# A decoder layer on one core: skip term written into PSUM by ScalarE, four slot products added by GpSimd

## What is computed

```python
xi, z = jnp.split(jnp.einsum('bld,ed->ble', xn, in_proj_w), 2, axis=-1)   # 1024 channels each
xc = silu(conv4(xi) + conv_b)
dt, Bm, Cm = jnp.split(jnp.einsum('bld,ed->ble', xc, x_proj_w), ...)
delta = softplus(dt @ dt_proj_w.T + dt_proj_b)
h[t] = exp(delta[t] * A) * h[t-1] + delta[t] * Bm[t] * xc[t]              # 16 states per channel
y = (h * Cm).sum(states) + xc * Dp                                        # xc * Dp is the skip term
y = y * silu(z);  out = y @ out_proj_w.T
```

## Time and profile before

| | |
|---|---|
| time, median of 3 runs | 2715.13 us (2707.16 to 2716.41) |
| the profiled execution: time, span | 2712.88 us, 2711.1 us |
| start, to the first u of step 0 | 79.6 us |
| 16 steps | 79.6 to about 1957 us |
| steps 4 to 13, each | 118.5 us |
| experts | 2030 to 2711 us |
| busy share of the span: PE, DVE, ACT, POOL | 93%, 78%, 63%, 61% |

### The profile page before, as it was taken

The page is one execution under the profiler, slowest core; times in us unless marked ns, Lnnn a source line. Parts: engine busy times, 40 slices in busy tenths (PEclk is TensorE's granted clock), DMA queues, the critical chain, the costliest instruction groups (busy, mean ns, idle before and its releaser), DMA issues.

```text
span 2711.1 us, 37373 instructions
## 1 busy us (share of the span) xinstructions
PE 2533.4 (93%) x11936; PEld 2179.8 (80%) x11936; DVE 2122.4 (78%) x2360; ACT 1714.0 (63%) x3891; POOL 1661.0 (61%) x980
## 2 busy tenths in 40 slices
PE   5689999999999999999999999998869999999997
PEld 5688888878888787888888788876649999999996
DVE  6899999989999998999899999998933454445442
ACT  4667787877777786877778777786643333333331
POOL 0878888878887988888788888888710100001100
PEclk9899999999999999999999999998879999999999
DMA  7123202122020212202020220202052332433320
GB/s 223 61 77 122 76 22 82 42 63 82 22 76 22 82 39 59 85 26 76 22 82 28 76 82 22 69 22 75 14 181 86 136 121 95 150 119 118 130 93 17
DMA packets 90907, 208.41 MB, mean 77 GB/s; under 512 B 7742, under 2 KB 16574, under 8 KB 90498
## 3 DMA queue, kind: packets, MB, share of 16 engines
q1 hardware_dynamic: 81506, 184.61, 21.6%
q0 software_dynamic: 5120, 14.21, 1.6%
q10 hardware_dynamic: 4096, 7.34, 0.9%
HBM read 176.69 MB, written 29.98 MB: 76 GB/s over the span
## 4 chain that ended last, share of the span: by engine, by line
PE 59%; DVE 13%; issue 9%; POOL 7%; ACT 7%; DMA 3%; SPq 1%; DVEq 0%; POOLq 0%; ACTq 0%
PE y L1511 14%; PE work L1525 12%; PE ring L1525 11%; PE work L1337 11%; DVE ring L1204 6%; POOL arena L929 3%; PE work L1358 3%; DVE arena L1213 3%; PE work L1374 2%; ACT ring L782 2%; DMA arena<-bc_rows 2%; DVE arena L1204 2%; PE work L1348 1%; POOL arena L934 1%; PE y L1508 1%
## 5 line engine op out<-in xcount | busy, mean ns | idle before, releaser
L929 POOL TENSOR_TENSOR arena<-arena 128x896 f32<-128x896 f32 x512 | 1058.5, 2090 | 221.8 <-PE y L1511 186.4
L782 ACT ACTIVATE ring<-arena,small 128x224 f32<-128x224 f32 x2048 | 795.7, 436 | 269.7 <-DVE arena L1213 229.6
L1511 PE MATMUL y<-arena,cst_sb 128*128 128x224 f32 x4096 | 857.5, 360 | 46.0 <-POOL arena L934 25.9
L1204 DVE TENSOR_TENSOR_SCAN ring<-ring,arena 128x896 f32<-128x896 f32 x400 | 809.2, 2023 | 93.1 <-ACT ring L782 51.4
L1511 PEld LDWEIGHTS y<-arena,cst_sb 128*128 128x128 f32 x4096 | 784.5, 194 | 104.0 <-issue 36.9
L947 POOL DMA_INDIRECT out<-res,ids x32 | 48.9, 1528 | 636.4 <-DVE mst L1261 554.1
L1213 DVE TENSOR_TENSOR arena<-ring,arena 128x896 f32<-128x896 f32 x400 | 433.2, 1083 | 5.4
L1337 PE MATMUL work<-arena 128*128 128x224 f32 x1984 | 406.5, 364 | 14.9 <-DVE slot_i L1109 8.9
L1337 PEld LDWEIGHTS work<-arena 128*128 128x128 f32 x1984 | 386.7, 197 | 23.3 <-DVE slot_i L1109 13.6
L1276 DVE SCALAR_TENSOR_TENSOR hidden_lo<-work,hidden_hi 128x448 fp32r<-128x448 f32 x128 | 80.0, 625 | 345.0 <-ACT hidden_hi L832 345.0
L832 ACT ACTIVATE hidden_hi<-work 128x448 fp32r<-128x448 f32 x128 | 69.8, 545 | 369.2 <-PE work L1525 369.2
(11 more groups left out here) (195 smaller groups left out, 3279.8 us busy)
## 6 DMA issues: line engine op xcount, KB each, us to landing
weights<-in_w SPq DMA_DIRECT2D x64, 1024.0 KB, 7.1
arena<-bc_rows SPq DMA_DIRECT2D x128, 448.0 KB, 4.5
arena<-in_ctx SPq DMA_DIRECT2D x16, 896.0 KB, 8.9
expert_rows<-x2e SPq DMA_DIRECT2D x1, 7224.0 KB, 29.8
xrow<-expert_rows SPq DMA_DIRECT2D x8, 903.0 KB, 11.7
arena<-in_xT SPq DMA_DIRECT2D x16, 448.0 KB, 9.5
arena<-in_x SPq DMA_DIRECT2D x16, 448.0 KB, 3.7
out<-arena ACTq DMA_DIRECT2D x32, 224.0 KB, 2.3
```

The source lines that it names most:

```text
L782: last = nc.scalar.activation(decays[s % 2][:, i * L:(i + 1) * L], delta[:, k, :], ACT.Exp, scale=a_neg[:, n:n + 1])
L929: nc.gpsimd.tensor_tensor(u[:, s % 4], dx[:, k:k + 1, :].to_broadcast([P, QN, L]), bc[:, 0, q * QN:(q + 1) * QN, :], ALU.mult).then_inc(u_ ...
L1204: nc.vector.tensor_tensor_scan(states, h, u_flat[:, s % 4, :], 0.0, ALU.mult, ALU.add).then_inc(scan_done, 1)
L1511: last = nc.tensor.matmul(o, ident, u[:, s % 4, i, :], start=False, stop=(q == Q - 1 and i == QN - 1))
```

## The change

1. **Skip term.** The matmuls of L1508, the tile `diag` and the 8 activations that built it in the start go. ACT writes `xc * D` straight into the PSUM bank of a channel pair (`skip_columns`, 2 activations of 128 x 224 for each of 4 pairs: jobs skip0 to skip3), after the gate has read the bank's last contents. PE waits for it (`skip_ready`) before the first sum of the pair, and all its sums accumulate onto it.
2. **Added products.** For slots 5, 9, 13 and 17 (`ADDED`) POOL, after its multiply, adds the product of the slot in front, in place. PE leaves out slots 4, 8, 12 and 16 and raises `sum_done` by two after the slot behind.
3. **A fifth u buffer**: buffer `s % 5` up to slot 19, `s % 4` from slot 20.
4. **Places.** All four tables, some banks and the orders of step -1 are new. In the start DVE's masks0 stands in the middle of the convolution, and ACT's silu stands ahead of the z copies.
5. w_x and w_dt get a semaphore of their own; PE's first xp waits for these two loads only, and others wait for the remaining six.

```diff
+    u_of = [s % 5 if s < 20 else s % 4 for s in range(SLOTS)]
...
+        ADDED = (5, 9, 13, 17)
...
+            def skip_columns(step, par, j):
+                if isinstance(step, int) and step == 0 and j < 2:
+                    act.wait_ge(w_free[2 + j], len(jobs_of[-1][2 + j]))
+                need(act, y_done, step * PAIRS + (j - 1))
+                if j == 0:
+                    act.wait_ge(xc_ready, step + 1)
+                for i in range(2):
+                    k = 2 * j + i
+                    last = nc.scalar.activation(yb[j % 2][:, i * L:(i + 1) * L], xc[:, par, k, :], ACT.Copy, scale=d_skip[:, k:k + 1])
+                last.then_inc(skip_ready, 1)
...
-                    for k in range(KB):
-                        nc.scalar.activation(diag[:, k, :], ident, ACT.Copy, scale=d_skip[:, k:k + 1]).then_inc(s_diag, 1)
...
-                    need(pool, sum_done, b * SLOTS + (s - 3))
+                    last = max((p for p in range(s) if u_of[p] == u_of[s]), default=max(p for p in range(SLOTS) if u_of[p] == u_of[s]) - SLOTS)
+                    need(pool, sum_done, b * SLOTS + (last + 1))
...
+                    if s - 2 in ADDED:
+                        pool.wait_ge(multiplied, b * len(ADDED) + (ADDED.index(s - 2) + 1))
+                        apart(pool)
+                        product_made(pool, b, s - 3)
+                        nc.gpsimd.tensor_tensor(u[:, u_of[s - 2]], u[:, u_of[s - 2]], u[:, u_of[s - 3]], ALU.add
                                                 ).then_inc(pooled_ready, 1)
...
                         if k % 2 == 0:
-                            need(pe, y_done, b * PAIRS + (k // 2 - 1))
-                        nc.tensor.matmul(o, diag[:, k, :], xc[:, par, k, :], start=True, stop=False)
+                            pe.wait_ge(skip_ready, b * PAIRS + (k // 2 + 1))
+                            apart(pe)
+                    if s + 1 in ADDED:
+                        return
                     product_made(pe, b, s)
                     for i in range(QN):
-                        last = nc.tensor.matmul(o, ident, u[:, s % 4, i, :], start=False, stop=(q == Q - 1 and i == QN - 1))
-                    last.then_inc(sum_done, 1)
+                        last = nc.tensor.matmul(o, ident, u[:, u_of[s], i, :], start=False, stop=(q == Q - 1 and i == QN - 1),
+                                                skip_group_check=True)
+                    last.then_inc(sum_done, 2 if s in ADDED else 1)
```

The places that matter below, before and after (the number is the slot):

```diff
-PE_AT   xi0-xi1: 0       xi2: 2         tx, rt, xi3: 3   out0.1-0.3: 7     out1.0: 8      out1.1-1.3: 10   z0, z1, plug: 16   z2, z3: 20
+PE_AT   xi0.0-xi1.0: 0   xi1.1, xi2: 1   tx, rt, xi3: 4   out0.1-out1.1: 7  out1.2-1.3: 9  z0.0-z1.0: 15    plug: 17   z1.1, z2, t1: 20   z3: 23
-POOL_AT delta1, delta2: 4   delta3: 11   scatter: 19   ctx: 20   delta0: 31   xn: 32
+POOL_AT delta1, delta2: 4   delta3: 12   scatter: 24   ctx: 30   delta0: 32   xn: 32.01
+ACT_AT  skip1: 9.01   skip2: 15   skip3: 26   skip0 (of the next step): 31
-DVE_FIRST ... conv2.1 conv2.2 conv2.3 conv3.1 conv3.2 conv3.3 masks0 masks1 ... masks7 corr0 ...
+DVE_FIRST ... conv2.1 masks0 conv2.2 conv2.3 conv3.1 conv3.2 conv3.3 masks1 ... masks7 corr0 ...
```

More of the change, by code:

```diff
@@ L45, in build_decoder @@
     SUB = QN * L
+    UB = 5
+    u_of = [s % 5 if s < 20 else s % 4 for s in range(SLOTS)]
     BIG_STEP = 1e28
@@ L73, in build_decoder @@
         for name, n in (
-            ("bc", 2 * NS * L), ("u", 4 * SUB), ("delta", KB * L), ("dx", KB * L), ("xc", 2 * KB * L),
+            ("bc", 2 * NS * L), ("u", UB * SUB), ("delta", KB * L), ("dx", KB * L), ("xc", 2 * KB * L),
             ("xT", DC * L), ("xn", DC * L), ("w1p", KB * L), ("sp3", 4 * L), ("w_in", DC * 2 * DI), ("gate", 2 * KB * L),
-            ("w_out", KB * D), ("w_x", KB * 3 * R), ("w_xa", DC * D), ("diag", KB * P),
+            ("w_out", KB * D), ("w_x", KB * 3 * R), ("w_xa", DC * D),
             ("x_res", 2 * D), ("r", 2 * D), ("hx", 2 * D), ("hT", 2 * DC * H), ("ctx", 2 * DCTX),
@@ L252, in apart @@
             eng.sem_inc(wait_kept, 1)
[L255 to L258, removed]
[5 rows of a table removed]
-        ACT_AT = {"norm2.0": 0, "tap0": 3, "tap1": 3.01, "norm2.1": 4, "tap2": 4.01, "tx0": 5, "tx1": 5.01, "tap3": 8,
[3 rows of a table removed]
-        DVE_AT = {"norm21.0": 1, "norm21.1": 2, "norm21.2": 3, "conv0.1": 3.01, "conv0.2": 3.02, "conv0.3": 3.03,
[6 rows of a table removed]
+        JOB_BANK = {"xi0": 0, "xi1": 1, "xi2": 0, "xi3": 1, "tx0": 1, "tx1": 0, "rt": 0, "rank": 1, "xp": 0, "out0": 0,
+                    "out1": 1, "dt0": 0, "dt1": 0, "dt2": 1, "dt3": 0, "z0": 1, "z1": 0, "z2": 1, "z3": 0, "t0": 1, "t1": 0,
+                    "plug": 1, "ssq": 1, "xatt0": 0, "xatt1": 1}
+        PE_AT = {"xi0.0": 0, "xi0.1": 0.01, "xi1.0": 0.02, "xi1.1": 1, "xi2.0": 1.01, "xi2.1": 1.02, "tx0": 4, "tx1": 4.01,
[5 rows of a table added]
+        ACT_AT = {"norm2.0": 1, "tap0": 3, "drop0": 3.01, "norm2.1": 4, "tap1": 4.01, "tap2": 4.02, "tx0": 5, "tx1": 5.01,
[3 rows of a table added]
+        DVE_AT = {"mask": 0, "norm21.0": 1, "norm21.1": 1.01, "norm21.2": 2, "conv0.1": 3, "conv0.2": 3.01, "conv0.3": 3.02,
[6 rows of a table added]
                   "norm20.2": 30.02}
-        POOL_AT = {"delta1": 4, "delta2": 4.01, "delta3": 11, "scatter": 19, "ctx": 20, "delta0": 31, "xn": 32}
+        POOL_AT = {"delta1": 4, "delta2": 4.01, "delta3": 12, "scatter": 24, "ctx": 30, "delta0": 32, "xn": 32.01}
         in_order = lambda names: {name: k for k, name in enumerate(names.split())}
@@ L279, in build_decoder @@
                                dt2 dt3 ssq""")
-        ACT_FIRST = in_order("""w_z skip tap0 tap1 tap2 tap3 z0 z1 z2 silu xp square z3 sp0 sp1 sp2 sp3 logs""")
-        DVE_FIRST = in_order("""conv0.1 conv0.2 conv0.3 conv1.1 conv1.2 conv1.3 conv2.1 conv2.2 conv2.3 conv3.1 conv3.2 conv3.3
-                                masks0 masks1 masks2 masks3 masks4 masks5 masks6 masks7 corr0 corr1 corr2 corr3""")
+        ACT_FIRST = in_order("""w_z tap0 tap1 tap2 tap3 silu z0 z1 z2 xp z3 sp0 sp1 sp2 sp3 square logs skip0""")
+        DVE_FIRST = in_order("""conv0.1 conv0.2 conv0.3 conv1.1 conv1.2 conv1.3 conv2.1 masks0 conv2.2 conv2.3 conv3.1 conv3.2
+                                conv3.3 masks1 masks2 masks3 masks4 masks5 masks6 masks7 corr0 corr1 corr2 corr3""")
         PE_DRAIN = in_order("""out0.0 out0.1 tx0 plug out0.2 out0.3 out1.0 out1.1 out1.2 out1.3 tx1 rt t0 rank t1 xatt0.0 xatt0.1
@@ L630, in last_tap @@
                 if j == 0 and (not isinstance(b, int) or b >= 1):
+                    act.wait_ge(skip_ready, b * PAIRS)
+                    apart(act)
                     act.wait_ge(sum_done, b * SLOTS - Q + 1)
@@ L672, in weights @@
                         nc.scalar.activation(w_in[:, c, DI:2 * DI], w_in[:, c, DI:2 * DI], ACT.Copy, scale=norm_w[:, c:c + 1]).then_inc(s_wz, 1)
-                    yield "skip"
-                    for k in range(KB):
-                        nc.scalar.activation(diag[:, k, :], ident, ACT.Copy, scale=d_skip[:, k:k + 1]).then_inc(s_diag, 1)
                 def rows():
@@ L758, in next_rows, with skips, first_skip @@
                     nc.scalar.activation(xn, xT, ACT.Square).then_inc(sq_ready, 1)
+                def skips():
+                    for j in range(1, PAIRS):
+                        yield f"skip{j}"
+                        skip_columns(b, par, j)
+                def first_skip():
+                    yield "skip0"
+                    skip_columns(nxt, 1 - par, 0)
                 def logarithms():
@@ L767, in side @@
                     (gate_inputs, pro), (residuals, epi), (context, epi), (depool, epi), (next_rows, pre), (logarithms, pre or pro),
-                    (weights, first)) if there))
+                    (weights, first), (skips, scan), (first_skip, pro)) if there))
             def body(b, par):
@@ L1179, in context_weights @@
                     yield "w_xa"
-                    dve.wait_ge(s_wrest, 16 * 8)
+                    dve.wait_ge(s_wrest, 16 * 6)
                     for c in range(DC):
@@ L1202, in main @@
                     h = decays[s % 2]
-                    states = u_flat[:, s % 4, :] if s in POOLED else h
-                    nc.vector.tensor_tensor_scan(states, h, u_flat[:, s % 4, :], 0.0, ALU.mult, ALU.add).then_inc(scan_done, 1)
+                    states = u_flat[:, u_of[s], :] if s in POOLED else h
+                    nc.vector.tensor_tensor_scan(states, h, u_flat[:, u_of[s], :], 0.0, ALU.mult, ALU.add).then_inc(scan_done, 1)
                 def product(s):
@@ L1353, in out_project @@
                 yield f"out{h}.0"
+                if isinstance(b, int) and b == 1 and h == 0:
+                    pe.wait_ge(s_wrest, 16 * 6)
                 bank, full = start_job(b, f"out{h}")
@@ L1417, in channels @@
                 if isinstance(b, int) and b == -1:
[L1418 removed]
+                    pe.wait_ge(s_wx, 16 * 2)
                 pe.wait_ge(xc_ready, nxt + 1)
```

37 lines of the change are left out of this document (15 added, 22 removed), and 28 rows, old and new, of tables (ACT_AT, DVE_AT, PE_AT).

## The result

The kernel after takes 2674.48 us (median of 4 runs, 2672.84 to 2675.49), the kernel before, in runs of the same sitting, 2712.58: a ratio of 0.985, interval 0.984 to 0.987. The forecast was 2686. The profiled execution took 2675.47 us with a span of 2673.7, so its span is 37.4 us shorter than before's 2711.1.

| stretch | before | after | difference | forecast |
|---|---|---|---|---|
| start, to the first u | 79.6 | 83.2 | +3.6 | +3.7 |
| steps 0 and 1 | 228.4 | 230.7 | +2.3 | 0 |
| steps 2 to 14 | 1535.5 | 1491.5 | -44.0 | -32.5 |
| step 15, drain, experts | 867.6 | 868.2 | +0.7 | 0 |
| one of steps 4 to 13 | 118.5 | 114.8 | -3.7 | -2.5 |

What follows compares the result with a forecast made beforehand. PE was taken to set the pace through the u buffers, DVE 4.5 us a step behind. 2712.9 - 32.5 (full steps) + 3.7 (start) = 2684.1, put at 2686 us for the median; range 2668 to 2702, chance 0.50.

Steps and rivals of the forecast that it cites:

- the odd stretches: Outside the full steps: start 3.7 us longer; steps 0, 1 and 15 between -3 and +3 each, counted as nothing.
- Drain and experts: The stretches after the steps: they keep their orders, so no change was counted.
- The loads: Busy time a step: PE 115.1 to 106.0 us, POOL 100.6 to 109.0, ACT 92.1 to 95.2, DVE unchanged at 110.6.
- The rival of a falling clock: In the steps, PE's granted clock falls, deciding below 0.91; at 0.89 a step of 121, total 2755 us; chance 0.06.
- the new step: Full steps 2 to 14: each falls from 118.5 to 116.0 us, saving 13 x 2.5 = 32.5 us.
- the two terms of the step: Drops in DVE's stalls a step: waits for POOL 2.7 to 1.0 (1.7 us), for ACT 3.8 to 3.0 (0.8 us).
- the stall behind silu: DVE's 2.10 us wait behind ACT's silu in a step: comes of ACT's own block and stays.
- The first paragraph of the prediction: In the full steps PE sets the pace through the u buffers; taking over some 4 us moves the bound to DVE.
- its paragraph on buffers and places: In a step, PE's bunches shorten or fall where no sum follows; POOL's 11.7 us of waiting for PE should mostly go.
- POOL becomes the bound: In the steps, over 3.0 of POOL's 11.7 us wait survives; with half, a step of 119.5, total 2738; chance 0.17.
- Two bounds coupled: In the steps DVE's idle of 7.9 us persists whatever frees PE; only the start counts, total 2719 us; chance 0.17.
- The hole at each add: After an added slot's scan, POOL needs 6.35 us against DVE's 6.2: about 0.15 us lost at each of four places.

Runs made afterwards that it cites:

- a_masks: Kernel after with masks0 moved back behind conv3.3 in the start: 2671.06 us, ratio 0.983 against the kernel before.
- a_oldplaces: Kernel after with the old tables of places and banks, the skip jobs added to ACT's old table: 2746.55 us, ratio 1.011 against the kernel before.
- a_noadd: Kernel after without POOL's four adds, PE summing all 32 slots: 2747.90 us, ratio 1.012 against the kernel before.
- b_u5: Kernel before with the fifth u buffer alone, all blocks using the diagonal of block 0: 2709.66 us, ratio 0.998.
- old_noadd: Kernel after with old places and no adds, leaving the skip term on ACT and the fifth buffer: 2728.89 us, ratio 1.005 against the kernel before.
- b_places: Kernel before with only the new tables of places and banks, the start's orders kept: 2772.44 us, ratio 1.021.
- b_pecut: Kernel before with three of four matmuls left out in the sums of eight slots a step: 2691.20 us, executed once.
- a_filler: a_masks with 8 small matmuls of 64 columns added on PE in each of slots 4, 8, 12 and 16: 2716.90 us, ratio 1.000 against the kernel before.
- a_pecut: Kernel after with two of four matmuls left out in the sums of eight slots a step: 2715.42 us, executed once.

## Why the prediction was right, and where it was not

**The direction and the odd stretches: right.** The start grew by 3.6 us, where 3.7 were worked out from the ten operations behind masks0, and `a_masks` took 3.2 of them back. Drain and experts moved by 0.7. Steps 0 and 1 grew by 2.3, inside the 3 each that was allowed.

**The loads: right but for PE.** POOL was forecast at 109.0 and is at 108.6, ACT 95.2 and 94.6. PE was forecast at 106.0 and is at 108.5. The matmuls are gone as counted (3584 instructions of L1540), but the granted clock over the ten steps is 0.97, not 0.99: 3% of 1148 us lost is about 34 us of full-clock work, against 12 in before's 1185 at 0.99. By these rounded clocks up to some 2 us more a step are lost, so the clock is probably most of the miss. The rival of a falling clock was right in direction and far from its point of 0.91.

**The term that was mis-sized: the new step.** It said 13 x 2.5 = 32.5 us; the measured term is 44.0. Of the prediction's waits, POOL's for PE went as said (under 3). But the two terms of the step, 1.7 and 0.8, were both off, and in opposite ways. DVE's waits for POOL were to fall from 2.7 to 1.0, the larger term; they fell to 1.75, so that freeing POOL from PE gave 0.9 and not 1.7. That the sum came near is in part luck, as the second term made up for the first. DVE's for ACT was to stay at 3.0, because the stall behind silu "comes of ACT's own block and stays". It did not stay: it is 1.1, so this term gave 2.7 and not 0.8. DVE in order of time in step 9 of the kernel after, where the earlier trace rows had 2.10:

```profile
1163.43 0.67 DVE L1087 SCALAR_TENSOR_TENSOR arena<-arena,work 112x512 f32<-112x512 f32 x1
1164.13 0.69 DVE L1033 BATCH_NORM_STATS2 st<-arena 112x6 f32<-112x512 f32 x1
1166.39 2.03 DVE L1235 TENSOR_TENSOR_SCAN ring<-ring,arena 128x896 f32<-128x896 f32 x1 [0.25 <-ACT ring L806]
1170.05 2.02 DVE L1235 TENSOR_TENSOR_SCAN arena<-ring,arena 128x896 f32<-128x896 f32 x1 [0.51 <-ACT ring L806]
```

The residual's side jobs (res0, L1087 and L1033) now stand in the same slot as ACT's silu. DVE does work that it owes anyway while ACT is away from the decays, and the stall shrinks to 0.25 and 0.51. I had read the tables for PE and POOL and not held DVE's against ACT's. `a_oldplaces` shows the other side: with the old tables the stall behind silu is 2.1 us again in a step such as step 9. Over steps 4 to 13 the silu stall falls from 2.1 to 0.8 us a step, which is half of the 2.7. The other half lies at other slots, and the tables alone don't bring it: with the same tables and no adds (`a_noadd`) DVE waits 7.8 us a step for ACT.

**A second part of the mis-sizing is the turn of the loop in the kernel before.** The prediction started from a mean of 118.5, but its ten steps are not alike. Steps 4, 5, 6 and 11, table of stretches of the kernel before, and the one wait of PE in steps 4 to 13 that the earlier trace rows leaves out:

```profile
543.90:664.40 120.50, 115.68 (x540) 97.28 (x539) 111.19 (x120) 92.75 (x226) 100.68 (x61) 0.99 0.19 54
664.40:780.70 116.30, 113.75 (x540) 95.81 (x539) 110.36 (x120) 91.09 (x222) 100.51 (x59) 1.00 0.20 57
780.70:902.80 122.10, 117.18 (x540) 98.76 (x539) 111.38 (x120) 92.92 (x226) 100.68 (x61) 0.97 0.18 54
1379.60:1496.70 117.10, 115.29 (x540) 97.41 (x539) 109.64 (x120) 92.08 (x224) 100.56 (x61) 0.99 0.18 56
```

```profile
PE y L1508 <- issue: 8.7, 4, 2.4
```

The long steps are 4, 6, 8 and 10 (120.5 to 122.3 us), each the first of a turn. In each of them, and in no other of the ten, PE stops for 1.8 to 2.4 us in front of the step's first matmul of L1508, with nothing in the profile that it waits for. DVE stands 3.0 us before the step's first scan in these steps and 0.6 in the others. The clock alone is not the reason: steps 4 and 11 both had 0.99, and step 4 took 3.4 us more. In the kernel after, PE has no such stop. At this place it waits some 1 us for DVE's first product in both kinds of step, and they are equally long (114.6 and 114.5). So 2.2 us are gained in a second step of a turn, 0.3 in a step that is written out (step 12 fell to a clock of 0.94), and most of the rest of the gain is that the turn no longer lengthens a step. With the old places it still does: in `b_u5` first and second steps take 120.4 and 117.0, in `old_noadd` 125.0 and 116.6, and the same wait of PE there:

```profile
PE y L1509 <- issue: 8.2, 4, 2.2
PE y L1540 <- issue: 17.2, 4, 4.5
```

In `b_places` the two kinds differ by 0.9 us only and the stop is 0.6 us in all; in `a_oldplaces` they differ by 1.5 and the wait has no entry. So either the new places or the adds take most of the turn's cost away, and each without the other costs more elsewhere than it gives. The prediction had no term for this.

**Dips of the clock.** PE's matmuls show what a dip is. The same 16 instructions of xi3, in order of time in steps 5 and 4 of the kernel before, run at either level of the clock:

```profile
688.73 3.27 PE L1337 MATMUL work<-arena 128*128 128x224 f32 x16
```

```profile
568.64 0.60 PE L1321 MATMUL work<-cst_sb,x2e 112*128 112x112 f32 x4 [1.07 <-ACT arena L603]
569.16 1.74 PE L1400 MATMUL work<-wr_sb,arena 128*112 128x8 f32 x16
570.76 4.96 PE L1337 MATMUL work<-arena 128*128 128x224 f32 x16
```

3.27 us for 16 is full clock, 2.4 GHz; 4.96 is partly 1.2 GHz. In front of it PE waited 1.07 us and then ran the sixteen instructions of 8 columns in 1.74; in step 5, where nothing fell, it waited 1.07 and ran them in 1.74 as well. Likewise the 8 instructions of L1511 behind PE's stop at the turn took 2.27 and 2.41 us in steps 6 and 8, but 1.76 and 1.78 in steps 4 and 10, after stops of 2.27, 2.45, 2.17 and 1.83 us.

The Trainium skill, "TensorE: Matmul & The Clock Gate", section "HAM oscillation — how this bites in real kernels", ties such a slow group to a wait for data in front of it; here the wait in front of the slow group is the same as in front of the fast one, so that wait alone doesn't decide it, and no run here shows what does.

**What was wrong in the reasoning though the number held.** The first paragraph of the prediction says that PE sets the pace, and that taking more than some 4 us from it moves the bound to DVE. That reads as if 9.1 us off PE would yield the gain by itself. `b_pecut` took 9.1 off and got 0.6; `b_u5` freed buffers and got nothing; the places alone cost 4.4. Of the versions that keep all the sums, only those with the adds, the fifth buffer and the places together gain more than 0.2%. The reading that fits is that the adds open four slots in which PE has no sum of its own, the places put long bunches of PE into these slots (five pieces of out-projection behind slot 7), and the fifth buffer keeps POOL ahead while the added pair holds two buffers. The prediction named this in its paragraph on buffers and places ("there the next slot has no sum of its own") but counted it as support rather than as the condition.

**The rivals.** "POOL becomes the bound" needed more than 3.0 of the 11.7 us of waiting to survive; 1.75 did. "Two bounds coupled" is half true. After the change, 6 us less on POOL give 0.5 a step and 6 us less on DVE give 0.9: neither engine bounds alone. DVE's idle, 7.9 us a step before, is 4.5 now, not 0. The hole at each add was forecast at 0.15 us; the add waits 0.23 us (9.1 / 40) for its multiply where 0.08 was taken. Whether that costs anything isn't shown.

**What stays open.** What starts each dip of the clock, and what PE's stop at the turn of the loop is. That dips lengthen steps rests on steps of the same work (`a_filler`: 116.5 at 1.00, 119.1 at 0.97) and on `a_pecut`, where less PE work came with a lower clock and a longer step; no run changed the clock and nothing else, and `a_filler` changed PE's load with it. The skip term was never put back on PE with the rest of the change kept, so its share of the gain isn't known. Which single place carries the gain wasn't tried, nor whether a version without adds would reach 114.8 with places fitted to it.

## What to carry to other kernels

Where engines run in lock step over a few buffers, ask of an engine's wait not only how busy the releaser is but what stands in front of the releasing instruction in its list; removing work elsewhere in that list can give next to nothing (9 us off PE gave 0.6). An edit that opens a gap and an order that uses the gap are one edit: measured apart, the parts here read from -0.2% to +2.1%, and a kernel that lacks one of them +1.1% to +6.8%, while together they give -1.5%. Before a stall is called fixed, look whether its victim has work of its own that could stand there. And before a mean over steps is taken as the start of a sum, look at the steps one by one, by their place in the loop: here the mean of 118.5 stood for steps of 121.5 and of 116.7.

## What the runs showed of the hardware that wasn't expected

Less work for PE made the kernel slower. With half of the sums of eight slots left out, PE's granted clock over steps 4 to 13 fell from 0.97 to 0.93, its busy time by 12 us where 60 us of work had gone, and the step grew from 114.8 to 118.1 us (one execution). Dummy matmuls brought the clock to 0.99 and were no gain: eight of 64 columns took 1.90 us.

The turn of a hardware loop wasn't free. A step that stands first in a turn took 4.8 us more than a second one in the kernel before and 8.4 us more in `old_noadd`, with PE stopped for 1.8 to 4.5 us and nothing shown that it waits for. In the kernel after the difference is 0.1 us.

The clock also varies from step to step of the same work: 0.99 and 0.94 in neighbouring steps of the kernel after (113.9 and 118.1 us), 1.00 and 0.97 in `a_filler` (116.5 and 119.1).

POOL's add, multiply and u all cost 2.09 us at 128 x 896, as before, although DVE was now busy for 96% of the step and not 93%. A skip activation into PSUM has a mean of 433 ns, against 436 for a decay.
